# Group means of a GroupNorm by 32x32 transposes and sums of eight on VectorE, in place of two small products on TensorE

## The reference

```
# x: (16, 256, 56, 56) float32, weight: (4, 256, 256, 3, 3), att_w: (4, 256), att_b: (4,)
def _gn(v, G=32, eps=1e-5):
    g = v.reshape(B_, G, C_ // G, H_, W_)
    m = mean(g, axis=(2, 3, 4)); s = var(g, axis=(2, 3, 4))
    return ((g - m) / sqrt(s + eps)).reshape(v.shape)

h = _gn(x)
pooled = mean(h, axis=(2, 3))
att = sigmoid(pooled @ att_w.T + att_b)            # one weight per sample and set
agg_w = einsum('nk,kocij->nocij', att, weight)     # a 3x3 kernel of its own for each sample
out = x + conv3x3(h, agg_w, padding=1)             # sample by sample
```

## Time and profile before

| | |
|---|---|
| time before, three runs | 1400.5, 1401.36, 1401.96 us, median 1401.36 |
| the profiled execution | 1404.19 us, of it the span 1402.6 us |
| busy in the span | PE 1296.8 us (92%), DVE 1186.8 us (85%), ACT 925.5 us (66%), POOL 59.1 us (4%) |
| chain that ended last | PE 73%, DVE 14%, issue 11% (time in which nothing in the profile was waited for), ACT 1% |
| granted clock of TensorE | 0.988 of full speed over the span |
| from the first convolution group to the last | 94.55 to some 1385 us, 16 epochs |

### The profile page before, as it was taken

How to read it: one execution, slowest core, us unless ns; L and a number is a source line. 1 busy time by engine, 2 the same in 40 slices (tenths; PEclk the granted TensorE clock), 3 DMA queues, 4 the chain that set the end, 5 groups by cost and what they waited for, 6 DMA issues and landing times.

```text
span 1402.6 us, 25344 instructions
## 1 busy us (share of the span) xinstructions
PE 1296.8 (92%) x8808; PEld 731.3 (52%) x8808; DVE 1186.8 (85%) x2000; ACT 925.5 (66%) x1466; POOL 59.1 (4%) x77
## 2 busy tenths in 40 slices
PE   0259999999999999999999999999999999999995
PEld 0125555555555555555555555555555555555552
DVE  3998898889988898888988898988988899898951
ACT  6666776677676767767676777667676766676520
POOL 0000000000000000000000000000000000000000
PEclk9979999999999999999999999999999999999998
DMA  9020455533445544433555344445543344553334
GB/s 363 2 93 6 134 139 139 127 82 115 118 117 139 139 126 108 107 100 116 138 139 139 90 111 123 103 130 138 139 119 90 110 111 127 139 138 93 92 88 96
DMA packets 29373, 165.70 MB, mean 118 GB/s; under 512 B 3360, under 2 KB 3616, under 8 KB 28192
## 3 DMA queue, kind: packets, MB, share of 16 engines
q1 hardware_dynamic: 20000, 112.34, 21.9%
q0 software_dynamic: 9216, 51.38, 21.7%
HBM read 112.33 MB, written 51.38 MB: 117 GB/s over the span
## 4 chain that ended last, share of the span: by engine, by line
PE 73%; DVE 14%; issue 11%; ACT 1%; DVEq 0%; POOL 0%; POOLq 0%; ACTq 0%
PE pM L399 66%; PE pG L374 6%; DVE Us L543 2%; DVE T L492 2%; DVE E L533 2%; DVE T L527 2%; DVE Vs L549 1%; DVE X L608 1%; DVE W L745 1%; DVE X L620 1%; DVE E L518 1%; DVE E L492 1%; DVE TB L601 0%; DVE TA L601 0%; PE pS L360 0%
## 5 line engine op out<-in xcount | busy, mean ns | idle before, releaser
L399 PE MATMUL pM<-Vs,Us 128*128 128x392 f16 x6912 | 1185.3, 332 | 26.8 <-DVE Us L543 14.1
L399 PEld LDWEIGHTS pM<-Vs,Us 128*128 128x128 f16 x6912 | 670.6, 98 | 530.4 <-issue 46.4
L790 ACT CAST Vs<-E 128x784 f16<-128x784 f32 x192 | 157.0, 844 | 166.5 <-DVE E L518 76.7
L492 DVE SCALAR_TENSOR_TENSOR T<-X 128x392 f32<-128x392 f32 x384 | 193.6, 558 | 7.6 <-ACT X L835 7.0
L549 DVE TENSOR_TENSOR Vs<-E,Vs 128x784 f16<-128x784 f32 x192 | 183.3, 970 | 0.7
L818 ACT ACTIVATE X<-pM,small 128x392 f32<-128x392 f32 x128 | 75.1, 587 | 118.0 <-PE pM L399 117.9
L800 ACT CAST Us<-E 128x768 f16<-128x768 f32 x128 | 102.9, 828 | 73.6 <-PE pM L399 41.6
L543 DVE SCALAR_TENSOR_TENSOR Us<-E,Us 128x768 f16<-128x768 f32 x128 | 119.1, 951 | 32.2 <-issue 29.9
L374 PE MATMUL pG<-W,D 128*32 128x512 f16 x1728 | 105.5, 390 | 31.4 <-DVE W L745 31.4
L856 ACT ACTIVATE unused<-X,small 128x784 bf16<-128x784 f32 x128 | 121.4, 949 | 6.3
L518 DVE SCALAR_TENSOR_TENSOR E<-T 128x784 f32<-128x784 f32 x128 | 119.1, 971 | 4.1
(11 more groups left out here) (72 smaller groups left out, 555.4 us busy)
## 6 DMA issues: line engine op xcount, KB each, us to landing
X<-x_dram SPq DMA_DIRECT2D x64, 784.0 KB, 5.4
X<-x_dram POOLq DMA_DIRECT2D x64, 784.0 KB, 8.2
out_dram<-X SPq DMA_DIRECT2D x64, 784.0 KB, 3.8
W<-w_dram SPq DMA_DIRECT2D x6, 1152.0 KB, 19.5
X<-w_dram SPq DMA_DIRECT2D x2, 1152.0 KB, 27.0
attw<-attw_dram SPq DMA_DIRECT2D x1, 128.0 KB, 8.5
small<-attb_dram SPq DMA_DIRECT2D x1, 0.5 KB, 10.8
```

The costliest lines, as they stand in the source:

```text
L399: mm = pe.matmul(tile_rows(bank(k, o)), Us[:, j, a, c, o, kx, :], v_in(j, b, c, kx), start=(at < 2 and n == 0), stop=(n == 3 * KS * CT - 1 ...
L492: ins = dve.scalar_tensor_tensor(out=dst[c], in0=a[c], scalar=scale, in1=d[c], op0=ALU.mult, op1=ALU.add)
L790: act.copy(v_out(j, 0), e_planes(("V", *v))).then_inc(v_hi, 1)
```

## The change

The two products on TensorE and the matrix `avg` go. Instead a channel's two numbers lie in columns 0 and 1 of a tile `col` of 128x32, the other columns of which are zeroed once. VectorE transposes the four 32x32 blocks of the tile, so the channels of a block lie along the free dimension; it sums eights (`tensor_reduce` to 128x4), writes each sum back eight times, scaled, with one `tensor_scalar` whose input is broadcast, and transposes back. This is done twice, for the mean and for the variance. GpSimd no longer builds `avg`, and its semaphore `sel_set` takes the place of `avg_set` for `attention(0)`. TensorE has two waits fewer in an epoch. The rest of the order is as before. The count of VectorE's held steps in an epoch goes from 29 to 36.

```diff
 @block.tensor
-            def group_mean_mm(e):
-                pe.wait_ge(mean_ready, e + 1)
-                pe.matmul(pS[:, 0:CT], avg[:, :], mv[:, :, 0], start=True, stop=True).then_inc(group_mean, 1)
-
-            def group_var_mm(e):
-                pe.wait_ge(spread_ready, e + 1)
-                pe.matmul(pS[:, CT:2 * CT], avg[:, :], spread[:, :], start=True, stop=True).then_inc(group_var, 1)
...
                 group(e, 5, 1)
-                if more:
-                    group_mean_mm(e)
                 group(e, 6, 0)
-                if more:
-                    group_var_mm(e)
                 group(e, 6, 1)
...
 @block.vector
+            def group_sums(e):
+
+                step(e, dve.transpose(colT[:, :], col[:, :]))
+                step(e, dve.tensor_reduce(sums8[:, :], eights(colT), AX.X, ALU.add))
+                return sums8[:, :].unsqueeze(2).broadcast_to([P, CI // GS, GS])
+
+            def eights(ap):
+                return ap[:, :].rearrange("p (g j) -> p g j", j=GS)
+
             def group_shift(e):
-                dve.wait_ge(group_mean, e + 1)
-                step(e, dve.tensor_scalar(nmean[:, :], pS[:, 0:CT], -1.0, None, ALU.mult))
-                step(e, dve.tensor_tensor(off[:, :], mv[:, :, 0], nmean[:, :], ALU.add))
+                dve.wait_ge(mean_ready, e + 1)
+                sums = group_sums(e)
+                step(e, dve.tensor_scalar(eights(colT), sums, -1.0 / GS, None, ALU.mult))
+                step(e, dve.transpose(nmean32[:, :], colT[:, :]))
+                step(e, dve.tensor_tensor(off[:, :], mean, nmean, ALU.add))
                 step(e, dve.tensor_tensor(sq[:, :], off[:, :], off[:, :], ALU.mult))
-                dve.tensor_tensor(spread[:, :], sq[:, :], mv[:, :, 1], ALU.add).then_inc(spread_ready, 1)
+                step(e, dve.tensor_tensor(spread, sq[:, :], own[:, :], ALU.add))
 
             def group_variance(e):
-                dve.wait_ge(group_var, e + 1)
-                dve.tensor_scalar(var[:, :], pS[:, CT:2 * CT], EPS, None, ALU.add).then_inc(var_ready, 1)
+                sums = group_sums(e)
+                step(e, dve.tensor_scalar(eights(colT), sums, 1.0 / GS, EPS, ALU.mult, ALU.add))
+                dve.transpose(var32[:, :], colT[:, :]).then_inc(var_ready, 1)
...
-            STEPS = 29
+            STEPS = 36
...
+            dve.memset(col[:, :], 0.0).then_inc(pads_set, 1)
```

More of the change, by code:

```diff
@@ L147, in conv_kernel @@
         TB = sb("TB", [P, CT, U], F32)
-        avg = sb("avg", [P, P], F32)
+        col = sb("col", [P, CI], F32)
+        colT = sb("colT", [P, CI], F32)
+        nmean32 = sb("nmean32", [P, CI], F32)
+        var32 = sb("var32", [P, CI], F32)
         sel = sb("sel", [P, CI], F32)
@@ L163, in conv_kernel @@
         unused = sb("unused", [P, CR * W // 2], mybir.dt.bfloat16)
-        mv = sb("mv", [P, CT, 2], F32)
-        nmean = small[:, 28:30]
+        mean = col[:, 0:CT]
+        spread = col[:, 0:CT]
+        nmean = nmean32[:, 0:CT]
+        var = var32[:, 0:CT]
+        own = small[:, 28:30]
         rstd = small[:, 30:32]
@@ L169, in conv_kernel @@
         sq = small[:, 36:38]
-        spread = small[:, 38:40]
-        var = small[:, 40:42]
+        sums8 = small[:, 38:42]
         std0 = small[:, 42:44]
@@ L199, in conv_kernel @@
         bias_set = sem("bias_set")
-        avg_set = sem("avg_set")
+        sel_set = sem("sel_set")
         pool_step = sem("pool_step")
@@ L458, in _ @@
             keep_clock(16)
-            pe.wait_ge(pads_set, 1)
+            pe.wait_ge(pads_set, 2)
             with pe.Fori(0, (N - 2) // 2) as i:
@@ L555, in channel_stats @@
                 step(e, dve.tensor_reduce(total[:, :], s1[:, :, :], AX.X, ALU.add))
-                step(e, dve.tensor_scalar(mv[:, :, 0], total[:, :], 1.0 / (H * W), None, ALU.mult))
-                step(e, dve.tensor_tensor(off[:, :], mv[:, :, 0], nk[:, :], ALU.add))
+                step(e, dve.tensor_scalar(mean, total[:, :], 1.0 / (H * W), None, ALU.mult))
+                step(e, dve.tensor_tensor(off[:, :], mean, nk[:, :], ALU.add))
                 step(e, dve.tensor_tensor(sq[:, :], off[:, :], off[:, :], ALU.mult))
@@ L559, in channel_stats @@
                 step(e, dve.tensor_reduce(total[:, :], s2[:, :, :], AX.X, ALU.add))
-                dve.scalar_tensor_tensor(out=mv[:, :, 1], in0=total[:, :], scalar=1.0 / (H * W), in1=sq[:, :],
+                dve.scalar_tensor_tensor(out=own[:, :], in0=total[:, :], scalar=1.0 / (H * W), in1=sq[:, :],
                                          op0=ALU.mult, op1=ALU.subtract).then_inc(mean_ready, 1)
-            def group_shift(e):
-                dve.wait_ge(group_mean, e + 1)
-                step(e, dve.tensor_scalar(nmean[:, :], pS[:, 0:CT], -1.0, None, ALU.mult))
-                step(e, dve.tensor_tensor(off[:, :], mv[:, :, 0], nmean[:, :], ALU.add))
+            def group_sums(e):
+                step(e, dve.transpose(colT[:, :], col[:, :]))
+                step(e, dve.tensor_reduce(sums8[:, :], eights(colT), AX.X, ALU.add))
+                return sums8[:, :].unsqueeze(2).broadcast_to([P, CI // GS, GS])
@@ L577, in norm_scale @@
                 step(e, dve.reciprocal(rs0[:, :], std0[:, :]))
-                step(e, dve.tensor_tensor(quo[:, :], var[:, :], rs0[:, :], ALU.mult))
+                step(e, dve.tensor_tensor(quo[:, :], var, rs0[:, :], ALU.mult))
                 step(e, dve.tensor_tensor(std[:, :], quo[:, :], std0[:, :], ALU.add))
@@ L724, in _ @@
             w_max(3)
-            dve.wait_ge(avg_set, 1)
+            dve.wait_ge(sel_set, K)
             attention(0)
@@ L993, in _ @@
             for k in range(K):
+                if k:
+                    pool.wait_ge(sel_set, k)
                 pool.affine_select(out=sel[:, :], in_=sel[:, :], compare_op=ALU.not_equal, fill=1.0, base=-CI * k,
[L995 to L1004 removed]
+                                   pattern=[[-1, CI]], channel_multiplier=1).then_inc(sel_set, 1)
             pool.wait_ge(w_top, 1)
```

22 lines of the change are left out of this document (3 added, 19 removed).

## The result

| | before | change |
|---|---|---|
| median | 1401.66 us (1400.5 to 1404.75, four runs) | 1411.62 us (1411.01 to 1412.46, four runs) |
| ratio, 95% interval | | 1.0065, 1.0049 to 1.0081 |
| the profiled execution, its span | 1404.19, 1402.6 us | 1411.01, 1409.3 us |

The change makes the kernel slower, by 0.65%. The side was the forecast one and the time lies in the range of 1401 to 1414 us, but the +10 us of the medians are twice the +4.8 us of the sum. The time also lies outside the forecast's own 1404.2 to 1410 us, and inside the 1411 to 1419 us of rival A, whose mechanism, dear transposes, is not what the trace shows. Where the rest comes from is the subject of what follows.

A forecast was written before the change was run, and what follows sets the result against it. VectorE, later than TensorE at nearly every loop end, was taken to bound the kernel. Passes +3.95 and +0.44, tail -0.49 and prologue +0.87 gave +4.8 us: 1406.2 us, range 1401 to 1414, the forecast's own 1404.2 to 1410.

The forecast's parts named there:

- rival A: VectorE's transposes are dear, each 0.35 us or more: +10 us or more, 1411 to 1419 us; chance 0.16.
- Prologue: VectorE's from 22 to 47 us, a delay there is paid less 0.68 us of wait for TensorE: +0.87 us.
- tail: Behind the last loop end nothing pins TensorE to VectorE: +0.07 for epoch 13, -0.28 each for 14 and 15, -0.49 us.
- first pass: Its first half has more slack and gains 0.28 us, its second half loses 0.72: +0.44 us.
- five passes: Passes beginning at a loop end where VectorE was late: +0.79 us each (+0.07 and +0.72 by halves), +3.95 us together.
- the six stops: VectorE's standstills at six loop ends, 29.9 us in all, 5.0 each, taken to stay as before.
- d1: VectorE's added delay from the statistics in a pass's first half: 1.55 us.
- the first half without a gain: TensorE's 0.28 us relief is lost to waits of 0.24 for `D` and 0.11 before `group(e, 11, 1)`: +0.07 us.
- d2: VectorE's added delay in a pass's second half, where 0.15 us of wait for TensorE goes: 1.40 us.
- what a second half forgives: VectorE's 0.68 us wait at `take_pair(9, 0)` absorbs that much of the 1.40 us delay, leaving 0.72 us.
- The delay ends at VectorE's 1.74 us wait, just big enough.: VectorE's wait at 686.42 us, before the second half's statistics, was to absorb the first half's whole delay.
- Rival C: VectorE's longer list shortens the loop-end stop by more than 2.6 us each: -10.1 us, about 1391; chance 0.09.

The follow-up runs named there:

- e2: Kernel before without its two products, VectorE using each channel's own mean and spread, same number of operations: 1400.19 us, ratio 0.9966.
- e1: Kernel before, products kept, with three spare held VectorE operations ahead of each of the two reads of a product: 1415.56 us, ratio 1.0077.
- e6: Changed kernel with VectorE's loop written out: 1392.87 us, ratio 0.9920 to the kernel before.
- e11: Changed kernel with the loops of VectorE, TensorE and ScalarE written out: 1386.20 us, ratio 0.9866 to the kernel before.
- e4: The change again: changed kernel unaltered, timed and traced a second time: 1413.72 us, ratio 1.0063 to the kernel before.
- e7: Changed kernel with one pair of transposes for both statistics, variance as mean of squares less square of the mean: 1403.71 us, ratio 0.9991 to before.
- e8: e7 with the loops of VectorE, TensorE and ScalarE written out: 1384.99 us, ratio 0.9863 to the kernel before.
- e3: Half of the change: against the kernel before, only the variance goes to VectorE, the mean stays a product: 1403.18 us, ratio 0.9989.
- e5: Kernel before with VectorE's loop written out: 1394.7 us, ratio 0.9936.
- e9: Before again: kernel before unaltered, timed and traced a second time: 1404.40 us, ratio 0.9997.
- e10: Kernel before with the loops of VectorE, TensorE and ScalarE written out: 1388.52 us, ratio 0.9884.

## Why the prediction was right, and what was mis-sized

In us, from TensorE's timeline of two pairs of traces. "Prologue" is the time to the first group, "passes" are the five between loop ends, less the stops, "tail" is from the last `group(e, 5, 0)` behind a loop end to the end of the span.

| | predicted | change - before | change again - before again |
|---|---|---|---|
| prologue | +0.87 | +0.90 | +1.00 |
| first pass, less its stop | +0.44 | -0.85 | +0.47 |
| five passes, less their stops | +3.95 | +4.61 | +5.42 |
| the six stops | 0 | +1.46 | +1.98 |
| tail | -0.49 | +0.56 | +1.16 |
| span | +4.8 | +6.7 | +10.0 |

**Right.** VectorE is the later engine at the loop ends, and what it carries into them is paid: e2 shows the relief without the delay and e1's second halves the delay without the relief, e6 and e11 take the ends away and the sign turns. The price of a transpose (0.204 and 0.211 us for 0.23), d1 (1.57 for 1.55), the first half without a gain (+0.11 for +0.07), the 2.5 us of wait at the loop end (2.4) and the prologue held. The first half's number holds by its sum only: of the two forecast waits one is shorter and one is not there, and a third was not seen. d2 is in the table of passes too: `D` in the second half starts at 100.83 where the statistics start at 83.48, 17.35 us, and before 99.36 - 83.37 = 15.99, so d2 is 1.36 for 1.40.

**Right for partly the wrong reason.** That no operation of VectorE is shorter than 0.16 us was misread, without effect (line 742 in the prologue takes 0.145). d1 is a sum of errors. The stretch of the mean grew by 0.93 us (1.78 for 0.85) where 0.775 was taken, because of the idle piece before `take_edge` (0.31 for 0.12) and although the four operations of a mean take 0.05 less than taken; from the variance's first operation to line 577 the growth is 0.68 (1.66 for 0.98), where 0.775 was taken. The time's place in the range is luck in part, too: about half of the loss comes from terms that stood at zero or below, and the range was wide enough only because it took in part of rival A. Two of the prediction's own signs of being wrong did appear: the stops at the loop's end changed (31.3 us for 29.9), and one held operation, the last ahead of `take_edge`, costs more than its length plus 0.035 (0.47 us start to start, 0.16 long).

**Mis-sized: what a second half forgives.** The 0.68 us wait is worth more than its length. It is counted from the end of the operation before, but where nothing is waited for the next take starts 0.08 us before that end: 730.50 and 731.04, each 0.62 long. So `D` comes 1.47 us late and this take 0.71, that is 0.76 forgiven, and another 0.05 is made up until the stop. This is why a pass whose load is in time costs +0.66 and not +0.79.

**Wrong: "The delay ends at VectorE's 1.74 us wait, just big enough."** On VectorE it does, but it had already left by `take_edge` to GpSimd, SyncE and the load of the next sample, and comes back over ScalarE's sums. This is the missing term of a pass: +0.79 was forecast, +0.66 is what a pass costs where the load is in time, and +0.92 and +1.08 are the means over five passes in the two traces. It is why the five passes gave +4.6 and +5.4. That the load is the way is read from traces, ten passes that fit one slack of 0.42 us, and e1, where three of the five passes wait, 0.21, 0.50 and 0.34 us, and only the one over 0.42 is longer, 158.80 us against 158.74 in the other four. No run took this way away alone, but in e6 and e11, where TensorE is the bound, the waits for loads are gone. Why some passes wait 0.12 and others 1.11 us for the same kind of load was not settled.

**Wrong: the tail.** -0.49 was forecast. The relief is there: two epochs, from the end of one's mixes at 1146.18 us to 1305.59, take 159.41 us where they took 159.96, and TensorE ends 282.2 us after the tail's begin in both traces of the change, 282.6 in both of before. What outweighs it is the last store of the output. The last GpSimd transfer lands 8.4 and 8.7 us after its issue, 8.5 and 8.2 in the two traces of before. Behind it the stretch from 1398.9 to 1402.5 us of before has

```profile
out_dram<-X SPq DMA_DIRECT2D x1, 784.0 KB, 3.2
```

and that from 1404.6 to 1409.2 us of the change

```profile
q14 instruction: 1, 0.01, 0.4%
...
out_dram<-X SPq DMA_DIRECT2D x1, 784.0 KB, 4.2
```

so the store lands 1.0 us later. This is no accident of one execution: the six traces of the change and of kernels made from it (e4, e6, e7, e8, e11) all have 4.2 us and one packet of the instruction queue in this stretch, and the seven of before and of kernels made from it (e1, e2, e3, e5, e9, e10) have 3.2 and none. So the tail is longer with the change's list of instructions and not with its products or its delay. Whether the fetch holds the store up, or only comes with what does, no run shows.

**Not in the sum: the stops.** I took them as unchanged. The single stop varies from 3.2 to 6.0 us within one kernel (e7), and six of them add up to 29.9 and 30.9 us in before, 31.3 and 32.9 in the change, 32.4 in e3 and 32.1 in e7. The first trace of before had a short one, and before again has one of 4.10; in the change, the change again and e1 none is under 4.95, with 18 stops in all. In before and its second trace, e2, e3 and e7 six of 30 are under 4.5. The times say the same: 12 executions of before again spread over 4.6 us and those of e3 and e7 over 7 each, while the change's spread over 1.5 (4) and 1.2 (5) and e1's over 1.6 (5); e2's 5 are as close, though (1.7). So the short stops seem to be rare where VectorE carries the whole delay, and on the mean of two traces each this is worth 1.7 us of the loss. Rival C, a stop that changes with VectorE's list, is then not refuted, but it is under a fifth of the loss, and why the short stops are missing stays open.

**The first pass** differs between the pairs by the granted clock, not by the change. In windows of 1 us, where the PEclk column is the third from the end, before has

```profile
99.00:100.00 1.00, 1.00 (x4) 0.44 (x3) 0.00 (x0) 1.00 (x3) 0.00 (x0) 0.50 0.00 0
100.00:101.00 1.00, 1.00 (x7) 0.58 (x6) 0.47 (x1) 1.00 (x2) 0.00 (x0) 0.98 0.00 0
```

and the change

```profile
98.00:99.00 1.00, 1.00 (x6) 0.50 (x5) 1.00 (x2) 0.97 (x3) 0.00 (x0) 0.70 0.00 0
99.00:100.00 1.00, 1.00 (x7) 0.57 (x6) 0.78 (x1) 1.00 (x3) 0.00 (x0) 1.00 0.00 0
```

so TensorE went from the lower of its two levels, 1.2 GHz, to 2.4 some 1.5 us later in that trace of before, though its first group began 0.9 us sooner (94.55 against 95.45). The second trace of before has the rise at 97 us, and there the first pass fits the forecast, +0.47 for +0.44. That the clock's rise accounts for the rest is worked out from the two traces of before: 5.5 us of the first pass lie at the lower level in the one trace of before, 2.7 in the other, and half of the difference is 1.4, where the passes differ by 1.3.

## What to carry to other kernels

When work is moved off the busiest engine, look for the places where the two engines meet in a strict order, such as a loop end: the one that arrives later there pays for every addition, however busy the other is, and what each place forgives is about the length of the wait that stands in front of it. Follow the delay over every operation that frees a buffer, too, through store and load and back, as slack on the engine itself says nothing of that way. Taking away the meeting place (the loops written out, 16 us) was worth more here than any work moved between the engines (2 to 4 us).

## What the runs showed of the hardware

- A 128x32 fp32 transpose in blocks on VectorE lasts 204 ns where the next one waits for it and 211 ns at the end of a chain, hardly more than the 128x32 cast (181 ns).
- VectorE stands still for 3.2 to 6.1 us where its loop closes, with no wait in the profile, and not at all when the loop is written out. In 46 of 48 such stops an 8 KB packet of the instruction queue starts 1.9 to 2.1 us before the engine goes on. Six such stops cost 9.6 us of their 30 where TensorE then became the bound.
- Idle pieces of about 0.3 us sit at fixed places of VectorE's list, such as ahead of line 545 in the first halves and ahead of `take_edge` in the change; before had them ahead of another `take_edge` in the first halves and ahead of line 582 in the second. They move with the list of instructions, and most are named as a wait for the instruction just before, although the pair of lines 544 and 545 runs 0.03 us apart in the second halves.
- A wait in VectorE's timeline is counted from the end of the operation before, but an operation that waits for nothing starts some 0.08 us before that end (0.62 us takes are 0.54 apart). A wait of 0.68 us forgave 0.76.
- The last store of 784 KB lands in 3.2 us in seven traces and in 4.2 in six, and in these six alone an instruction packet moves between its issue and its landing.
